# Second expert's split reordered over ScalarE, VectorE and POOL; an own order for the last steps; the routing weights' broadcast in four transfers

## The reference

```python
x = L0_attn_x                                   # (8, 2048, 256)
# attention, over y = layernorm(x)
Q, K, V = y @ wq.T, y @ wk.T, y @ wv.T           # D = 64
energy = einsum('bnd,bne->bde', K, V)            # one 64x64 matrix per sequence
x = x + (einsum('bnd,bde->bne', Q, energy) * sqrt(3/64)) @ wo.T
# ffn, over h = layernorm(x)
scores = sigmoid(h @ Wr)                         # 8 scores, the best 2 (with bias) kept
cw = the two kept scores, divided by their sum   # at most 2 of 8 are not zero
routed = sum over the 4 experts e: cw[e] * ((silu(h @ Wg[e]) * (h @ Wu[e])) @ Wd[e])
routed += (cw[4] + cw[6]) * h + cw[7] * relu(h)
shared = causal depthwise conv over 4 tokens (h) + conv_b
x = x + routed + shared
```

## Time and profile before

| | us |
|---|---|
| median of 3 runs | 924.8 (924.77 to 928.49) |
| the profiled execution | 928.5 |
| its span in the trace | 926.7 |

### The profile page before, as it was taken

The page is one execution under the profiler, slowest core; times in us unless marked ns, Lnnn a source line. Parts: engine busy times, 40 slices in busy tenths (PEclk is TensorE's granted clock), DMA queues, the critical chain, the costliest instruction groups (busy, mean ns, idle before and its releaser), DMA issues.

```text
span 926.7 us, 16363 instructions
## 1 busy us (share of the span) xinstructions
PE 881.6 (95%) x5402; PEld 767.2 (83%) x5402; DVE 690.0 (74%) x1998; ACT 602.5 (65%) x1212; POOL 608.5 (66%) x686
## 2 busy tenths in 40 slices
PE   5779999999999999999999999999999999988896
PEld 4668888888888888888898888888888888777785
DVE  5766878977787888778779877877887776666563
ACT  5675676677677667766766776676677656644543
POOL 3236776667677666777766676786667767665663
PEclk9888999999999999999999999999999999999999
DMA  9111434434234443334344442434443322333232
GB/s 288 42 69 29 130 116 137 138 115 122 62 123 128 138 137 114 102 90 129 115 138 138 119 132 52 132 115 138 137 117 113 92 69 93 112 115 107 77 92 67
DMA packets 65620, 103.83 MB, mean 112 GB/s; under 512 B 4992, under 2 KB 57344, under 8 KB 61440
## 3 DMA queue, kind: packets, MB, share of 16 engines
q1 hardware_dynamic: 60928, 86.01, 27.4%
q0 software_dynamic: 4608, 16.78, 9.6%
HBM read 68.96 MB, written 17.04 MB: 93 GB/s over the span
## 4 chain that ended last, share of the span: by engine, by line
PE 53%; POOL 31%; DVE 5%; ACT 5%; issue 4%; DMA 1%; POOLq 0%; ACTq 0%; DVEq 0%
POOL enx L1287 17%; POOL gate L1254 8%; PE ps_gu L391 6%; PE ps_gu L393 6%; PE ps_gu L392 6%; PE ps_gram L457 6%; PE ps_y L391 5%; PE ps_y L392 4%; PE ps_y L393 4%; POOL hid_lo L1259 4%; PE ps_sh L482 3%; PE ps_gram L459 3%; PE ps_sh L499 3%; ACT gate L720 2%; PE ps_gu L532 2%
## 5 line engine op out<-in xcount | busy, mean ns | idle before, releaser
L1254 POOL TENSOR_TENSOR gate<-gate,cwb 128x512 f32<-128x512 f32 x128 | 165.3, 1292 | 113.8 <-ACT gate L720 74.8
L391 PE MATMUL ps_gu<-x2T_hi,wgu_hi 128*128 128x512 f32 x512 | 212.2, 414 | 3.3 <-DVE hid L956 3.3
L393 PE MATMUL ps_gu<-x2T_hi,wgu_lo 128*128 128x512 f32 x512 | 203.2, 397 | 0.0
L392 PE MATMUL ps_gu<-x2T_lo,wgu_hi 128*128 128x512 f32 x512 | 202.4, 395 | 0.0
L1287 POOL TENSOR_TENSOR enx<-inv_e,logits 128x32 f32<-128x32 f32 x32 | 177.1, 5535 | 10.6 <-ACT logits L713 10.4
L956 DVE TENSOR_TENSOR hid<-ps_gu,gate 128x512 f32<-128x512 f32 x128 | 86.2, 673 | 123.8 <-POOL gate L1254 101.7
L391 PE MATMUL ps_y<-wd_hi,hid_hi 128*128 128x256 f32 x512 | 157.2, 307 | 6.6 <-POOL hid_lo L1259 3.1
L393 PE MATMUL ps_y<-wd_hi,hid_lo 128*128 128x256 f32 x512 | 145.8, 285 | 0.0
L392 PE MATMUL ps_y<-wd_lo,hid_hi 128*128 128x256 f32 x512 | 145.8, 285 | 0.0
L973 DVE SCALAR_TENSOR_TENSOR conv<-x2T,conv_w,conv 128x512 f32<-128x512 f32 x192 | 144.2, 789 | 0.0
L391 PEld LDWEIGHTS ps_gu<-x2T_hi,wgu_hi 128*128 128x128 f32 x512 | 97.3, 190 | 22.7 <-DVE hid L956 6.8
(11 more groups left out here) (103 smaller groups left out, 1837.6 us busy)
## 6 DMA issues: line engine op xcount, KB each, us to landing
cwb<-cw_rows SPq DMA_DIRECT2D x32, 1024.0 KB, 4.7
xa<-in_x SPq DMA_DIRECT2D x32, 512.0 KB, 6.9
acc<-in_x SPq DMA_DIRECT2D x32, 512.0 KB, 6.0
acc<-x POOLq DMA_DIRECT2D x32, 512.0 KB, 4.6
out<-acc SPq DMA_DIRECT2D x64, 256.0 KB, 2.3
cwb<-in_wg SPq DMA_DIRECT2D x4, 128.0 KB, 3.8
cwb<-in_wu SPq DMA_DIRECT2D x4, 128.0 KB, 3.6
cwb<-in_wd SPq DMA_DIRECT2D x1, 512.0 KB, 4.5
```

What stands on the lines that cost most here:

```text
L391: nc.tensor.matmul(dst, a_hi, b_hi, start=start, stop=False, skip_group_check=True)
L392: nc.tensor.matmul(dst, a_hi, b_lo, start=False, stop=False, skip_group_check=True)
L393: return nc.tensor.matmul(dst, a_lo, b_hi, start=False, stop=stop, skip_group_check=True)
L1254: g.tensor_tensor(gate[:, e % 2], gate[:, e % 2], cwb[:, q, e], ALU.mult).then_inc(gatew_ready, 1)
```

## The change

A new method `Step.drain()` is true where C has a group, A has none, and the step is not the first B step of a sequence: steps 34 to 38. The change has four parts.

1. In every step ScalarE's `hid_high(st, 1)` stands right behind `silu(st, 2)`, ahead of the scalings and relus, and `hid_low(st, 1)` goes from POOL to VectorE, ahead of `hidden(st, 2)`.
2. In the steps of `drain()` that have a B (34, 35, 36), TensorE's attention halves stand around `gate_up(st, 4)`, VectorE's residual and statistics ahead of `hidden(st, 2)` and the route, POOL's relu DMA and norm factors ahead of `gate_weight(st, 3)`, and ScalarE's `norm2` ahead of `hid_high(st, 3)`.
3. In step 37, which has R and C but no B, `route` stands ahead of `hidden(st, 2)`.
4. The broadcast of the routing weights is four DMAs, one for each expert, each with its own semaphore, and each `gate_weight` waits for its own.

The method and SP:

```diff
+    def drain(self):
+        return self.on("C") and not self.on("A") and not self.chain()
...
-                sp.dma_start(cwb[:, k].rearrange("p e n -> p (e n)"),
-                             rows.rearrange("a e n -> (a e n)").partition_broadcast(P))\
-                    .then_inc(cwb_loaded[k], 16)
+                for e in range(EM):
+                    sp.dma_start(cwb[:, k, e], rows[0, e].partition_broadcast(P)).then_inc(cwb_loaded[k][e], 16)
```

TensorE:

```diff
                     chain_f(st)
+                if b_on and drain:
+                    attention(st, 0)
                 if c_on:
                     gate_up(st, 4)
+                if b_on and drain:
+                    attention(st, 1)
                 if c_on:
                     conv_transpose(st)
                     down(st, "C", 0)
-                if b_on and not m_on:
+                if b_on and not m_on and not drain:
                     attention(st, 0)
...
-                if b_on:
+                if b_on and not drain:
                     attention(st, 1)
```

ScalarE:

```diff
                 if c_on:
                     silu(st, 2)
+                    hid_high(st, 1)
...
                             .then_inc(relu_ready, 1)
-                    hid_high(st, 1)
...
                     weights_copy(st)
+                if st.on("B") and st.drain():
+                    norm2(st)
...
                     xnT_high(st, 1)
-                if st.on("B"):
+                if st.on("B") and not st.drain():
                     norm2(st)
```

VectorE:

```diff
                     f_low(st)
+                drain = st.drain()
+                if c_on:
+                    hid_low(st, 1)
+                if b_on and drain:
+                    residual(st, 0)
+                    residual(st, 1)
+                    norm2_stats(st)
+                if r_on and c_on and not b_on:
+                    route(st)
                 if c_on:
                     hidden(st, 2)
-                if r_on and c_on:
+                if r_on and c_on and b_on:
                     route(st)
                 if c_on:
                     hid_low(st, 2)
-                if b_on:
+                if b_on and not drain:
                     residual(st, 0)
                     residual(st, 1)
                     norm2_stats(st)
```

POOL:

```diff
-                if e == 0:
-                    pool.wait_ge(cwb_loaded[q], st.uses("C", 2, 16, 16))
+                pool.wait_ge(cwb_loaded[q][e], st.uses("C", 2, 16, 16))
...
                     gate_weight(st, 2)
-                    hid_low(st, 1)
                     norm1_factors(st)
+                    if st.drain():
+                        relu_add(st)
+                        if st.on("B"):
+                            norm2_factors(st)
                     gate_weight(st, 3)
-                if c_on:
-
-                    pool.wait_ge(ident_added, st.before("C", TG, TG))
-                    pool.wait_ge(relu_ready, st.before("C", TG, TG))
...
-                if st.on("B"):
+                if c_on and not st.drain():
+                    relu_add(st)
+                if st.on("B") and not st.drain():
                     norm2_factors(st)
```

More of the change, by code:

```diff
@@ L225, in program @@
         cw_stored = sem("cw_stored")
-        cwb_loaded = [sem(f"cwb_loaded{k}") for k in range(2)]
+        cwb_loaded = [[sem(f"cwb_loaded{k}_{e}") for e in range(EM)] for k in range(2)]
         zeroed = sem("zeroed")
@@ L961, in hid_low @@
                 dve.wait_ge(hidhi_ready, st.before("C", EM, e + 1))
-                v.tensor_tensor(hid_lo[:, 0], hid[:, 0], hid_hi[:, 0].bitcast(F32), ALU.subtract)\
-                    .then_inc(hidlo_ready[0], 1)
+                k = e % 2
+                v.tensor_tensor(hid_lo[:, k], hid[:, k], hid_hi[:, k].bitcast(F32), ALU.subtract)\
+                    .then_inc(hidlo_ready[k], 1)
             def conv_tap(st, n):
@@ L1250, in gate_weight, with last_low, relu_add @@
                 q = st.slot("C", 2)
-                if e == 0:
-                    pool.wait_ge(cwb_loaded[q], st.uses("C", 2, 16, 16))
+                pool.wait_ge(cwb_loaded[q][e], st.uses("C", 2, 16, 16))
                 pool.wait_ge(gate_ready, st.before("C", EM, e + 1))
                 g.tensor_tensor(gate[:, e % 2], gate[:, e % 2], cwb[:, q, e], ALU.mult).then_inc(gatew_ready, 1)
-            def hid_low(st, e):
-                pool.wait_ge(hidhi_ready, st.before("C", EM, e + 1))
+            def last_low(st):
+                pool.wait_ge(hidhi_ready, st.before("C", EM, EM))
                 g.tensor_tensor(hid_lo[:, 1], hid[:, 1], hid_hi[:, 1].bitcast(F32), ALU.subtract)\
                     .then_inc(hidlo_ready[1], 1)
+            def relu_add(st):
+                pool.wait_ge(ident_added, st.before("C", TG, TG))
+                pool.wait_ge(relu_ready, st.before("C", TG, TG))
+                k, q = st.slot("C", 4), st.slot("C", 2)
+                g.dma_start(acc[:, k].rearrange("p t n -> p (t n)"), x2[:, q].rearrange("p t n -> p (t n)"),
+                            accum_op=ALU.add).then_inc(relu_added[q], 16)
             def norm2_factors(st):
@@ L1309, in body @@
                     gate_weight(st, 2)
-                    hid_low(st, 1)
                     norm1_factors(st)
+                    if st.drain():
+                        relu_add(st)
+                        if st.on("B"):
+                            norm2_factors(st)
                     gate_weight(st, 3)
-                if c_on:
-                    pool.wait_ge(ident_added, st.before("C", TG, TG))
-                    pool.wait_ge(relu_ready, st.before("C", TG, TG))
-                    k, q = st.slot("C", 4), st.slot("C", 2)
-                    g.dma_start(acc[:, k].rearrange("p t n -> p (t n)"), x2[:, q].rearrange("p t n -> p (t n)"),
-                                accum_op=ALU.add).then_inc(relu_added[q], 16)
-                if st.on("B"):
+                if c_on and not st.drain():
+                    relu_add(st)
+                if st.on("B") and not st.drain():
                     norm2_factors(st)
                 if c_on:
-                    hid_low(st, 3)
+                    last_low(st)
                 if r_on:
```

## The result

The changed kernel takes 902.31 us (median of four runs, 901.47 to 906.31) against 926.24 for the one before, run beside it (924.77 to 928.49): a ratio of 0.9748, with an interval of 0.971 to 0.9786. The forecast was 899, in a range of 891 to 908. The profiled execution takes 902.03 us, its span is 900.2; that of before was 926.7, so the traces differ by 26.5 us and the medians by 23.9, where the sum had 25.3.

What follows compares the result with a forecast made beforehand. TensorE was taken to bound ordinary steps, and a loop with residual and norm behind the route the late ones. Gains 10.1 + 12.1 + 4.4 - 1.3 = 25.3 us from the 924.8 median give 899.5, stated as 899, range 891 to 908.

Steps and rivals of the forecast that it cites:

- second expert's halves, ordinary steps: Steps 8 to 33: TensorE's wait for POOL's low half goes, 0.39 us in each of 26 steps, 10.1 us.
- four transfers, ordinary steps: Outside the end, three more SP issues a step delay only loads of acc and x: taken as 0.
- late periods, with the clock: Steps 34 to 36: three periods of 23.4 us replace 82.3 us, gaining 12.1, less 1.3 for a clock fall.
- step 37 and the end: Step 37 taken as 0, bounds 0 and 1; the end gains 2.3, 1.7 and 0.4, sum 4.4 us.
- What bounds: TensorE sets the ordinary step, busy 25.89 of 26.00 us with one wait; something else sets the late steps.
- Clock: New late-step stops, 1.9 us in two pieces, may halve TensorE's clock: one of four steps charged, 1.3 us, bounds 0 and 5.2.
- The rule: Shared-port rule would hold VectorE's low half until POOL's power ends; the forecast instead kept it ready at T+5.0.
- The low half did not wait: Rival, 5%: the low half waits for POOL's power, costing 1.1 us in each of three late steps, 902.8 us.
- the wait did not come back: Rival, 10%: the wait removed from ordinary steps comes back elsewhere, the 10.1 us is lost, 909.6 us.
- the clock fell in two of four steps, not in all: Rival, 10%: TensorE's clock falls in every late step, four times 1.3 us instead of once, 903.4 us.
- nothing or little: Rival, 3%: clock, rule and returned wait come together, 921 us.
- More than the forecast: Rival, 7%: route freed of POOL's product, clock holds, last stops vanish; 4 to 7 us more, about 893 us.

Runs made afterwards that it cites:

- four transfers alone: The kernel before with only the weights' broadcast split into four transfers, each with its own semaphore: ratio 0.9962 to the kernel before.
- halves alone: The kernel before with only part 1, both the early high half and the low half on VectorE: ratio 0.9887 to the kernel before.
- one transfer again: The changed kernel with the weights' broadcast as a single transfer again: ratio 0.9777 to the kernel before.
- the low half alone: The kernel before with only the second expert's low half moved to VectorE, high half left behind relu: 918.77 us, ratio 0.9906.
- the kernel with the product moved: The changed kernel with POOL's fourth product in late steps waiting until VectorE's combine weights are ready: 896.01 us, ratio 0.9668 to the kernel before.
- the better kernel: The changed kernel with POOL's fourth product in late steps waiting until the combine weights are ready: 896.01 us, ratio 0.9668 to the kernel before.
- first quarter and rest: The changed kernel with the broadcast as two transfers, the first quarter and the other three together: 904.24 us, ratio 0.9751 to the kernel before.
- step 37's route back: The changed kernel with the route behind hidden(2) again in step 37: 903.82 us, ratio 0.9739 to the kernel before.
- the three kernels whose trace has the product moved: The changed kernel with POOL's fourth product behind the weights: alone 0.9668, with a gate matmul ahead of the weights' transpose 0.9665, with step 37's route behind hidden(2) 0.9662.

## Why the prediction was right, and where its terms were off

What 26.5 us of span consist of, from the distances of the powers. It is one trace against one; the medians differ by 23.9.

| term | forecast | measured |
|---|---|---|
| head and first body step | 0 | 2.2 |
| second expert's halves, ordinary steps | 10.1 | 8.9 |
| four transfers, ordinary steps | 0 | 2.2 |
| late periods, with the clock | 12.1 - 1.3 | 10.3 |
| step 33 | in the halves | 0.1 |
| step 37 and the end | 4.4 | 2.8 |

- *What bounds.* Right. The ordinary step is TensorE's, and once its one wait is gone it stands at 25.81 us.
- *Halves.* The mechanism is right: four steps 1.51 us shorter, forecast 1.6. The 0.39 per wait was 0.36 to 0.39. 8.9 is the difference between the ordinary periods of the kernel with four transfers alone and of the changed one. Counted the other way, the halves with one transfer give 6.0 (halves alone) to 7.4 (one transfer again) and the four transfers 3.7 to 5.2. Either way the halves are less than the 10.1, and the two terms together are 11.1. That the late high half is not the cause, but POOL as the engine of the low half, was not separated in the forecast; the low half alone shows it.
- *Four transfers elsewhere, "I take 0".* Wrong, on the gain's side, and it makes up for the halves, which is luck. I looked at what the issues cost and at gate(1), not at gate(0), whose late start falls on VectorE's taps: 2.2 us with the old halves, 3.7 or more with the new. That head and first body step were 2.2 us shorter is nothing that the runs can lay to the change: between these kernels the first power came at 46.28 to 50.73 us.
- *Late steps.* Period 23.49 for a forecast of 23.4, weights ready at 824.01, T+12.7 as forecast. Two errors cancel in it. Hid(2) began the route earlier (T+8.5 instead of 8.9), and the route took 4.21 us instead of the 3.85 that I carried over. The 3.85 was no bare duration either. In the kernel before it held waits beside POOL:

```profile
836.08 1.30 POOL L1259 TENSOR_TENSOR hid_lo<-hid,hid_hi 128x512 fp32r<-128x512 f32 x1 [0.33 <-ACT hid_hi L713]
...
836.77 0.66 DVE L1027 TENSOR_TENSOR biased<-score,bias 128x32 f32<-128x32 f32 x1
...
838.02 1.29 POOL L1254 TENSOR_TENSOR gate<-gate,cwb 128x512 f32<-128x512 f32 x1 [0.65 <-ACT gate L720]
...
838.87 0.49 DVE L1038 SCALAR_TENSOR_TENSOR raw<-marked,score 128x32 f32<-128x32 f32 x1
```

  Each ends where POOL's ends (837.4, 839.3); undisturbed they take 0.19 and 0.19. Free of such waits the route is 3.09 us (819.80 to 822.89 in the kernel with the product moved). Norm2 began at T+13.3, ahead of `hid_hi(3)`, and TensorE stopped at the weights' transpose, both as forecast.
- *Clock.* In the four steps 34 to 37 it fell twice, in step 36 and in step 37, where one fall was forecast. A fall in a late period cost 1.5 us, not 1.3: the 2.6 us at half speed in the forecast rest on no row, and 0.57 over 848 to 852 comes to about 3.4 us. A nearer row than the stops of 1.16 and 2.26 was there, in the same late step of the kernel before; the window behind it has a clock of 0.72:

```profile
847.95 0.73 PE L499 MATMUL ps_sh<-ident,x 128*128 128x128 f32 x2 [1.64 <-ACT x L792]
...
848.00:854.00 6.00, 5.72 (x27) 4.80 (x28) 2.08 (x4) 3.93 (x8) 2.33 (x6) 0.72 0.25 89
```

  The clock fell behind this stop in all three late steps of that trace. The old period of 27.4 thus held a fall, the new one was built at full speed, and the forecast did not say so.
- *Step 37 and the end.* Mis-sized: 2.8 for 4.4, and it is step 37, taken as 0 with a bound of 1, that took the difference. Its late `down(2)`, with the fall of the clock behind it, cost the 2.0 us that come back with the route behind hid(2). Behind it the end came as told: no stop for hid(0), full clock over 880 to 885. Step 38 has one stop left, 0.47 us at 892.39 for a low half. But the four transfers were not what gave it in this kernel: with one transfer again the end is 39.51, since hid(0) waits for VectorE's outputs. In the kernel before, they do give 3.6 (43.17 to 39.55).
- *The rule.* The low half ran inside the power, 815.50 in 811.29 to 816.73, in 0.69 us. So far the trace speaks against the Trainium skill's page "SBUF — State Buffer", section "SBUF: two separate sides". But the waits of `biased`, `raw`, `cw` and the taps beside POOL's products of 128x512 are of the kind that the section states, two inputs in SBUF, and that of `wsum_eps`, with one, is its other case, a mode that uses both ports. Moving the product removes that of `wsum_eps`, and with it the 1.11 us; that a port is the cause is the page's account, the runs show only what waits for what. I weighed the rule for one pair only, found that it did not hold there, and did not ask it of the others.
- *Rivals.* The low half did not wait; the wait did not come back; the clock fell in two of four steps, not in all. The 921 of "nothing or little" does not follow from its parts: 3.3, 3.9 and 10.1 on top of 899.5 make 916.8. "More than the forecast" named the route freed of POOL's product, which is what the better kernel then does.

## What to carry to other kernels

A duration carried over from the old trace holds the contention of its old neighbours: take the minimum of the instruction over the trace, and price what stands beside it in the new order separately. Put a long operation of GpSimd where VectorE runs no chain of small ones that something waits for; one semaphore wait did that here and gave 0.8%. For a transfer that many steps wait for, look at its slow landings, not only at the median, and at what the work that it releases then falls on; split off the part that is needed first (first quarter and rest did as well as four).

## What the runs showed of the hardware

- POOL's power (5.43 us, 128x32) held up no VectorE operation of 128x512 with two inputs in SBUF (0.69 us), while its plain product of 128x512 (1.27 us) held up VectorE operations of 128x4 and 128x32 until its end: 0.17 to 1.29 us, 0.22 to 1.28 us. POOL's product is longer too where it meets VectorE's low half (1.63 us at 822.97 in the kernel with the product moved).
- In the trace of the kernel before, some instructions of VectorE were held up each time and others never, when they began while POOL made a product or a low half of 128x512 (and over 0.25 us ahead of its end). Held were 31 of 31 `biased`, 25 of 25 `wsum_eps` and 6 of 6 `raw`; they ended with POOL's. Not held were `score` (24, at most 0.34 us) and `wsum` (25, at most 0.19), which have one input, and `hid` (12, at most 0.68), which has one of its two in PSUM. In the changed kernel 62 low halves on VectorE began inside a power, and all took 0.67 to 0.69.
- A fall of TensorE's clock cost 1.5 to 1.6 us each time in a step of the new orders (23.49 to 25.02, 26.39 to 27.96). In which step it came differed between kernels whose order in that step is the same: in step 33 the kernel with step 37's route back had one and the changed kernel none. What decides it there stays open. Behind stops of 1.35 and 0.30 us it came in step 36 of the changed kernel and not in 34 and 35; behind one of 1.69 us in step 37 it came; in steps 34 to 36 of the three kernels whose trace has the product moved, with stops of 0.92 us at most, it never came.
